# Reordering the spectral stage of a decoder kernel: correlation ahead of the lag transforms, two PSUM banks used differently, masked scores in PSUM

## The chip, the cores and the metric

The kernel runs on one core of one Trainium2 chip. The metric is the device time of one execution in microseconds, and each kernel is judged by the median of several runs. The engines are TensorE (PE; its weight loads are shown apart as PEld), VectorE (DVE), ScalarE (ACT) and GpSimd (POOL); SyncE (SP) issues the DMAs. Each engine works through its own list of instructions in order, and they meet only through semaphores.

## The reference

Everything is computed on 32 sequences of 64 tokens with 512 features, in float32:

```
x = x + attn_block(layernorm(x))      # dequantised weights + LoRA, then gate/up/down
x = x + autocorrelation(Q=layernorm(x), K=ctx, V=ctx)
x = x + top1_expert_lora(layernorm(x))

def autocorrelation(Q, K, V):         # 8 heads of 64 features, over the 64 positions
    corr = ifft(fft(q) * conj(fft(k))).real
    w, idx = top_k(corr, 8)           # per feature, over the lags
    w = softmax(w)
    out = sum_i w[i] * v[min(idx[i] + pos, L - 1)]
```

The last two lines of x, for 16 tiles of 128 tokens (two sequences each), are the spectral stage, which this change touches. The first line, some 690 us of the execution, is untouched.

## The kernel before, in words

The spectral stage is a software pipeline written out by hand. `slots` (L985) runs over slots v; in slot v an engine does stage s for tile t = v - s, so up to four tiles are under way. Each engine has its own `piece` function, from L1039 (SP), L1087 (POOL), L1156 (ACT), L1251 (DVE) and L1336 (PE), and the order of the calls there is the order of its queue. Nothing plans it: order and waits stand as written. Stage 0 of tile 0 runs earlier, between the last matmuls of the block before, so that the slots of PE, ACT, DVE and POOL begin at v = 1 and the last is v = 18.

Fourier transforms are matmuls by fixed 64-row matrices, one for each of the two sequences (`by_sequence`, L696, its matmuls on line L700). For one tile, in order:

- Stage 0. PE transforms ctx to kc (`pe_kc`) and ACT copies it out (`act_kc`, L739); PE transforms the normalised x (`pe_q`, from xq, which ACT made at L687); PE transforms ctx once more to kn (`pe_kn`), and ACT copies it (L745). DVE multiplies q by kc (`dve_product`, L755), and PE transforms back with the products as weights (`pe_corr`, L767). DVE takes the 8 largest of each row (`dve_top`, L782), subtracts the largest (L786, L788), ACT takes exponentials (`act_exp`, L803, L807), DVE sums (`dve_sum`, L813), POOL divides (`pool_divide`, L822, tile en), DVE marks the chosen lags (`dve_mark`, L797).
- Stage 1. DVE weighs (`dve_weigh`, L831, tile wl), PE transposes that (`pe_lags`, L843), ACT copies it to wts (`act_lags`, L865). PE transforms wts twice, `pe_cyclic` and `pe_negacyclic` (both L700); DVE multiplies the first by kc (`dve_cyclic`, L877), ACT copies the second (L871), and POOL multiplies it by kn (`pool_negacyclic`, L885, tile pn). PE transforms both products back into one sum (`pe_gather`, L896), and DVE adds x (`dve_x3`, L905).
- Stage 2. Layer norm of x3 (`dve_stats`, `pool_pow`, `dve_rstd`, ACT at L676), PE transposes it (`pe_turn_h`, L913), ACT copies it to x3t (L920), PE computes router logits and the low-rank products (`pe_route`, L928), DVE picks the expert (`dve_route`, L939 to L953: mx, sc, m2, rw, wh), PE transposes wh (`pe_turn_wh`, L960), ACT copies that to wht (`act_expert`, L971).
- Stage 3. PE multiplies wht by the expert matrix (`pe_expert`, L965), DVE adds it (`dve_final`, L977), and SP stores the tile.

PSUM has eight banks. CORR is bank 0, LAGS bank 1 (the transposed lags, and later in the same tile the gathered sum), QW banks 2 and 3 (q, then the cyclic transform), MISC bank 4 (transposed x, then the expert's output), ROUTE bank 5, KW banks 6 and 7 (kc, kn, negacyclic transform). A semaphore guards each reuse. PE's order in a slot is kc(v), q(v), lags(v-1), expert(v-3), kn(v), cyclic(v-1), negacyclic(v-1), corr(v), turn_h(v-2), route(v-2), gather(v-1) twice, turn_wh(v-2). The kn copy must precede the negacyclic transform, which writes over kn.

Of the kernel before, what the change touches and what calls it, by code (L numbers as in the profile page):

```python
# [97 lines left out]
def build(nc, x, ctx_in, codes, scale_nat, scale_rows, lora_attn, lora_h, lora_ft, lora_down_b,  # L98
# [91 lines left out]
    x3t = two("x3t")  # L190
    mx, sc, m2, rw = two("mx", (8,)), two("sc", (E,)), two("m2", (8,)), two("rw", (E,))
    wh, wht = two("wh", (P,)), two("wht", (P,))
# [5 lines left out]

    CORR, LAGS, QW, MISC, ROUTE, KW = 0, 1, 2, 4, 5, 6

# [509 lines left out]
    def pe_q(pe, t, b):  # L710
        pe.wait_ge(xq_done, t + 1)
        if t == 0:
            pe.wait_ge(kn_copied, 1)
        elif t == 1:
            pe.wait_ge(hmul_done, 2 * NG * NCH)
        else:
            pe.wait_ge(pcyc, t - 1)
        by_sequence(pe, q_bank(t), SPEC, xq[:, b]).then_inc(q_ready, 1)

    def pe_kc(pe, t, b, h):  # L720
        pe.wait_ge(ctx_in_s[b], 16 * h + 16)
        if t == 0:
            pe.wait_ge(const_in, 48)
            pe.wait_ge(folded, PER * NG)
        elif t == 1:
            pe.wait_ge(prod, 1)
        else:
            pe.wait_ge(wn_copied, t - 1)
        by_sequence(pe, KW, KCYC, ctx[:, b]).then_inc(kc_ready, 1)
# [45 lines left out]
    def dve_top(dve, t, b):  # L775

        corr = ps[:, CORR].rearrange("p (r l) -> p r l", l=L)
        dve.wait_ge(corr_ready, t + 1)
        if real(2 * (t - 1)):
            dve.wait_ge(exp_done, 2 * (t - 1))  # L780
# [28 lines left out]
    def dve_sum(dve, t, b):  # L809
        dve.wait_ge(exp_done, 2 * t + 1)  # L810
        if real(t - 1):
# [5 lines left out]
    def pool_divide(pool, t, b):  # L817
        pool.wait_ge(exp_done, 2 * t + 2)
        pool.wait_ge(summed, 2 * t + 2)
# [40 lines left out]
    def act_lags(act, t, b):  # L860
        act.wait_ge(lag_turned, t + 1)
        if real(t - 1):
            act.wait_ge(wc_ready, t - 1)
            act.wait_ge(wn_ready, t - 1)
        nc.scalar.copy(wts[:, b], ps[:, LAGS]).then_inc(lag_copied, 1)  # L865

# [20 lines left out]
    def pe_gather(pe, t, b, k):  # L887

        if k == 0:
            pe.wait_ge(lag_copied, t + 1)  # L890
            pe.wait_ge(pcyc, t + 1)
        else:
            pe.wait_ge(pneg, 2 * t + 2)
        mat, src = ((OUT, pc), (OUT_N, pn))[k]
        for s in range(2):
            mm = nc.tensor.matmul(ps[s * L:(s + 1) * L, LAGS], spec[:, mat, 0:L], src[:, b, s],  # L896
                                  start=(k == 0), stop=(k == 1))
# [3 lines left out]
    def dve_x3(dve, t, b):  # L901
        dve.wait_ge(gathered, t + 1)
        if real(t - 1):
            dve.wait_ge(fin_done, t - 1)
        nc.vector.tensor_tensor(x3[:, b], tile_of(acc, t), ps[:, LAGS], ALU.add).then_inc(x3_done, 1)  # L905

    def pe_turn_h(pe, t, b):
        pe.wait_ge(xh3_done, t + 1)
        if real(t):
            pe.wait_ge(fin_done, t)  # L910
        for j in range(KT):
# [20 lines left out]
    def dve_route(dve, t, b):  # L932

        logits = ps[:, ROUTE, P:P + E]
        n = 4 * t
        dve.wait_ge(routed_in, t + 1)
        if real(4 * (t - 1)):
# [3 lines left out]
        dve.wait_ge(prio_set, E)  # L941
        nc.vector.scalar_tensor_tensor(out=sc[:, b], in0=logits, scalar=mx[:, b, 0:1], in1=prio[:],
                                       op0=ALU.is_equal, op1=ALU.mult).then_inc(route, 1)
        dve.wait_ge(route, n + 2)
        nc.vector.max(m2[:, b], sc[:, b]).then_inc(route, 1)
        dve.wait_ge(route, n + 3)
        nc.vector.scalar_tensor_tensor(out=rw[:, b], in0=sc[:, b], scalar=m2[:, b, 0:1],
                                       in1=mx[:, b, 0:1].to_broadcast([P, E]), op0=ALU.is_equal,
# [35 lines left out]

    def slots(e, piece, first=1):  # L985


        for v in range(first, TT + DEEP):
            def at(stage):

                t = v - stage
                return (t, t % 2, t // 2) if 0 <= t < TT else None
            piece(at)
# [6 lines left out]
    with nc.Block() as block:  # L1000

        @block.sync
        def _(sp):
# [40 lines left out]
            slots(sp, piece, 0)  # L1044
            for b in range(2):
# [3 lines left out]
        def _(pool):  # L1049
# [37 lines left out]
            def piece(at):  # L1087
                if a := at(2):
                    pool_pow(pool, *a[:2])
                if a := at(1):  # L1090
                    pool_negacyclic(pool, *a[:2])
                if a := at(0):
                    pool_divide(pool, *a[:2])
            slots(pool, piece)

        @block.scalar
        def _(act):
# [20 lines left out]
            def body(g, gp, m, ahead):  # L1118
                for c in range(NCH):
# [19 lines left out]
                    else:  # L1139
# [12 lines left out]
            pairs(act, body)  # L1152
            act_exp(act, 0, 0)
            act.wait_ge(added, 4 * NCH * NG)

            def piece(at):  # L1156
                if a := at(0):
                    act_kc(act, *a[:2])
                if a := at(1):
                    act_lags(act, *a[:2])  # L1160
                if a := at(0):
                    act_kn(act, *a[:2])
# [4 lines left out]
                if a := at(2):  # L1167
                    act_turn_h(act, *a[:2])
                if a := at(-1):
                    act_normalise_x2(act, *a[:2])  # L1170
                if a := at(0):
                    act_exp(act, *a[:2])
# [5 lines left out]
        def _(dve):  # L1178
# [72 lines left out]
            def piece(at):  # L1251
                if a := at(1):
                    dve_weigh(dve, *a[:2])
                if a := at(2):
                    dve_stats(dve, *a[:2])
                if a := at(0):
                    dve_product(dve, *a[:2])
                if a := at(2):
                    dve_rstd(dve, *a[:2])
                if a := at(1):  # L1260
                    dve_cyclic(dve, *a[:2])
                if a := at(3):
                    dve_final(dve, *a)
                if a := at(0):
# [4 lines left out]
                if a := at(0):  # L1269
                    dve_mark(dve, *a[:2])  # L1270
# [5 lines left out]
        def _(pe):  # L1276
# [59 lines left out]
            def piece(at):  # L1336
                if a := at(0):
                    pe_kc(pe, *a)
                    pe_q(pe, *a[:2])
# [4 lines left out]
                if a := at(0):  # L1344
                    pe_kn(pe, *a[:2])
                if a := at(1):
                    pe_cyclic(pe, *a[:2])
                    pe_negacyclic(pe, *a[:2])
                if a := at(0):
                    pe_corr(pe, *a[:2])  # L1350
                if a := at(2):
                    pe_turn_h(pe, *a[:2])
                    pe_route(pe, *a[:2])
                if a := at(1):
                    pe_gather(pe, *a[:2], 0)
                    pe_gather(pe, *a[:2], 1)
                if a := at(2):
                    pe_turn_wh(pe, *a[:2])
            slots(pe, piece)
# [58 lines left out]
```

## Time and profile before

| | |
|---|---|
| median of 3 runs | 934.58 us (934.45, 934.58, 938.98) |
| the profiled execution | 935.97 us, span 934.2 us |
| busy over the span | PE 827.9, DVE 567.6, ACT 393.4, POOL 205.2 us |
| TensorE clock granted over the span | 0.97 |
| span of the spectral stage | from 691 us to the end |

The profile is of one execution. Each row of a timeline gives the start, the duration, the engine, the line of the code, the operation with its output and inputs, their shapes, how many instructions are merged into it, and in brackets how long the engine was idle before it and which instruction released it. Tiles are named without their buffer numbers; ps is any PSUM bank. "issue" is idle time for which the profile shows no releaser. A granted clock of 1.00 is 2.4 GHz.

### The profile page before, as it was taken

The page shows a single profiled execution, that of the slowest core. Times are in us where ns is not written, and L with a number is a line of the kernel's source. Part 1 is how long each engine was busy: PE and PEld are TensorE (multiplying, and loading weights), DVE is VectorE, ACT ScalarE, POOL GpSimd, SP SyncE. Part 2 cuts the span into 40 slices and gives each one's busy share as a digit, 9 for nine tenths or more (in the row PEclk, how much of TensorE's full clock was granted, in tenths as well). Part 3 has the DMA queues.
Part 4 walks back from the last instruction along what each step waited for, and adds up shares of the span by engine and source line. Part 5 has one row for each costly group of instructions (what it writes and reads, how often), then busy time and mean ns, then how long its engine had stood idle before and what let it go on. Part 6 is the DMA issues. An engine that isn't in the chain of part 4 may idle for free. (4 is left out here: it accounts for less than half of the span.)

```text
span 934.2 us, 10840 instructions
## 1 busy us (share of the span) xinstructions
PE 827.9 (89%) x3548; PEld 574.4 (61%) x3548; DVE 567.6 (61%) x1327; ACT 393.4 (42%) x675; POOL 205.2 (22%) x187
## 2 busy tenths in 40 slices
PE   2577769899999999999999999999968888888875
PEld 0233357677777777777777777787744434444432
DVE  3777556665456456456456456423467788787783
ACT  3666545544344344444443443211214444544431
POOL 2000001122222222222222222222113323223221
PEclk9799989999999999999999999999979999999997
DMA  5422111211111111111112111010000101101100
GB/s 157 127 71 78 45 51 31 69 49 50 45 49 49 46 47 50 46 39 58 46 38 61 46 38 45 1 66 1 11 1 12 45 24 46 46 24 46 39 19 34
DMA packets 26551, 43.06 MB, mean 46 GB/s; under 512 B 4368, under 2 KB 6576, under 8 KB 26496
## 3 DMA queue, kind: packets, MB, share of 16 engines
q1 hardware_dynamic: 26496, 42.37, 14.7%
q8 instruction: 29, 0.48, 0.2%
q14 instruction: 26, 0.21, 0.1%
HBM read 38.16 MB, written 4.19 MB: 45 GB/s over the span
## 5 line engine op out<-in xcount | busy, mean ns | idle before, releaser
L478 PE MATMUL ps<-x_hi,w_hi 128*128 128x512 f32 x448 | 189.9, 424 | 2.4 <-DVE x_lo L526 2.4
L480 PE MATMUL ps<-x_hi,w_lo 128*128 128x512 f32 x448 | 175.4, 392 | 0.0
L479 PE MATMUL ps<-x_lo,w_hi 128*128 128x512 f32 x448 | 175.1, 391 | 0.0
L602 DVE TENSOR_TENSOR acc<-acc,ps 128x512 f32<-128x512 f32 x112 | 75.7, 685 | 78.8 <-PE ps L480 78.8
L365 POOL TENSOR_TENSOR w_lo<-wt,w_hi 128x512 fp32r<-128x512 f32 x42 | 54.7, 1303 | 274.7 <-ACT w_hi L360 274.7
L593 POOL TENSOR_TENSOR h_lo<-hf,h_hi 128x512 fp32r<-128x512 f32 x56 | 72.1, 1287 | 177.7 <-ACT h_hi L588 177.4
L478 PEld LDWEIGHTS ps<-x_hi,w_hi 128*128 128x128 f32 x448 | 84.3, 188 | 30.2 <-issue 13.9
L581 DVE TENSOR_TENSOR hf<-hf,ps 128x512 f32<-128x512 f32 x56 | 38.4, 687 | 101.1 <-PE ps L480 101.1
L479 PEld LDWEIGHTS ps<-x_lo,w_hi 128*128 128x128 f32 x448 | 84.4, 188 | 25.2 <-issue 8.7
L480 PEld LDWEIGHTS ps<-x_hi,w_lo 128*128 128x128 f32 x448 | 84.4, 188 | 18.0
L575 ACT ACTIVATE hf<-ps 128x512 f32<-128x512 f32 x56 | 33.5, 597 | 143.7 <-PE ps L480 143.7
L478 PE MATMUL ps<-w_hi,h_hi 128*128 128x512 f32 x224 | 88.3, 394 | 4.1 <-DVE acc L602 4.1
L588 ACT CAST h_hi<-hf 128x512 fp32r<-128x512 f32 x56 | 34.7, 620 | 129.0 <-DVE hf L581 128.9
L479 PE MATMUL ps<-w_lo,h_hi 128*128 128x512 f32 x224 | 88.1, 393 | 0.0
L480 PE MATMUL ps<-w_hi,h_lo 128*128 128x512 f32 x224 | 88.0, 393 | 0.0
L453 PE MATMUL ps<-w,wt 128*128 128x512 f32 x96 | 49.1, 659 | 16.1 <-DVE wt L305 9.7
L885 POOL TENSOR_TENSOR pn<-wns,kn 128x512 f32<-128x512 f32 x32 | 40.0, 1270 | 73.8 <-ACT wns L871 73.8
L284 DVE SCALAR_TENSOR_TENSOR piece_c<-piece_c,piece_a 128x512 f32<-128x512 f32 x58 | 41.1, 709 | 22.2 <-ACT piece_c L273 18.4
L287 DVE SCALAR_TENSOR_TENSOR piece_d<-piece_d,piece_c 128x512 f32<-128x512 f32 x58 | 52.9, 912 | 2.0
L280 DVE SCALAR_TENSOR_TENSOR piece_a<-piece_a,piece_b 128x512 f32<-128x512 f32 x58 | 47.5, 819 | 10.7 <-ACT piece_b L267 10.1
L478 PEld LDWEIGHTS ps<-w_hi,h_hi 128*128 128x128 f32 x224 | 42.6, 190 | 13.4 <-issue 4.5
L351 DVE TENSOR_TENSOR wt<-wt,ps 128x512 f32<-128x512 f32 x42 | 28.7, 682 | 35.6 <-PE ps L320 35.6
(120 smaller groups left out, 1378.4 us busy)
## 6 DMA issues: line engine op xcount, KB each, us to landing
codes_sb<-in_codes SPq DMA_DIRECT2D x58, 256.0 KB, 2.6
scale_sb<-in_scale_rows SPq DMA_DIRECT2D x92, 128.0 KB, 2.9
acc<-in_x SPq DMA_DIRECT2D x4, 1024.0 KB, 5.8
ctx<-in_ctx SPq DMA_DIRECT2D x16, 256.0 KB, 2.6
out<-fin SPq DMA_DIRECT2D x16, 256.0 KB, 2.0
lft<-in_lora_ft SPq DMA_DIRECT2D x56, 16.0 KB, 1.9
spec<-in_spectral SPq DMA_DIRECT2D x1, 448.0 KB, 3.3
rt<-in_router SPq DMA_DIRECT2D x1, 272.0 KB, 3.6
```

The source lines that it names most:

```text
L280: nc.vector.scalar_tensor_tensor(out=piece_a[:, b], in0=piece_a[:, b], scalar=KA, in1=piece_b[:, b], op0=ALU.add, op1=ALU.min).then_inc(mi ...
L284: nc.vector.scalar_tensor_tensor(out=piece_c[:, b], in0=piece_c[:, b], scalar=-SHIFT, in1=piece_a[:, b], op0=ALU.add, op1=ALU.min).then_in ...
L287: nc.vector.scalar_tensor_tensor(out=piece_d[:, b], in0=piece_d[:, b], scalar=KD, in1=piece_c[:, b], op0=ALU.add, op1=ALU.max).then_inc(mi ...
L365: nc.gpsimd.tensor_tensor(w_lo[gp][:, k], wt[:, b], w_hi[gp][:, k].bitcast(F32), ALU.subtract).then_inc(lo_done, 1)
L453: mm = nc.tensor.matmul(ps[:, kt, :], wt[:, u % 2, kt * P:(kt + 1) * P], w3[:, o], start=(u == KT), stop=False)
L478: nc.tensor.matmul(bank, hi, rhs_hi, start=start, stop=False)
L479: nc.tensor.matmul(bank, hi, rhs_lo, start=False, stop=False)
L480: return nc.tensor.matmul(bank, lo, rhs_hi, start=False, stop=stop)
L581: nc.vector.tensor_tensor(hf[:, i], hf[:, i], ps[:, 2 * i + 1], ALU.mult).then_inc(hmul_done, 1)
L593: nc.gpsimd.tensor_tensor(h_lo[:, c % 2, i], hf[:, i], h_hi[:, c % 2, i].bitcast(F32), ALU.subtract).then_inc(hlo_done, 1)
L602: nc.vector.tensor_tensor(tile, tile, ps[:, 4 + s % 2], ALU.add).then_inc(added, 1)
L885: nc.gpsimd.tensor_tensor(pn[:, b, s], wns[:, b, s], kn[:, b, s], ALU.mult).then_inc(pneg, 1)
```

## The change

What it does, part by part:

- The transposed lags go to bank MISC instead of bank 1, and bank 1 (now named GATHER) holds only the gathered sum. `pe_lags` waits for the x3t copy of an earlier tile instead of for x3; `pe_gather` waits for x3; and `pe_expert(v-3)`, which writes MISC, waits for the wts copy of tile v-1.
- PE's new order is kc(v), q(v), turn_wh(v-3), lags(v-1), expert(v-3), kn(v), corr(v), negacyclic(v-1), cyclic(v-1), turn_h(v-2), route(v-2), gather twice. So turn_wh moves into the next slot.
- DVE's new order is weigh, product, stats, rstd, final, top, cyclic, sum, route, mark, x3.
- ACT's order is the same; the exponential of the top values has a semaphore of its own, `top_exp`.
- The masked scores sc of `dve_route` are in PSUM (bank ROUTE) instead of SBUF.
- SP loads ctx a slot earlier. POOL's calls are written in another order with other stages (`pool_pow` for tile v-1 at the end of slot v instead of tile v-2 at its start), which gives the same queue.

```diff
-    CORR, LAGS, QW, MISC, ROUTE, KW = 0, 1, 2, 4, 5, 6
+    CORR, GATHER, QW, MISC, ROUTE, KW = 0, 1, 2, 4, 5, 6
...
-    def act_exp(act, t, b):
+    def act_exp_top(act, t, b):
         act.wait_ge(topd_done, t + 1)
         flat = topd[:, b].rearrange("p r k -> p (r k)")
-        nc.scalar.activation(flat, flat, ACT.Exp).then_inc(exp_done, 1)
+        nc.scalar.activation(flat, flat, ACT.Exp).then_inc(top_exp, 1)
+
+    def act_exp(act, t, b):
         act.wait_ge(less_done, t + 1)
...
     def dve_sum(dve, t, b):
-        dve.wait_ge(exp_done, 2 * t + 1)
+        dve.wait_ge(top_exp, t + 1)
...
     def pe_lags(pe, t, b):
...
-        if real(t):
-            pe.wait_ge(x3_done, t)
+        if real(t - 1):
+            pe.wait_ge(h_copied, t - 1)
...
-            mm = nc.tensor.transpose(ps[:, LAGS, ch], wl[:, b, ch], eye[:])
+            mm = nc.tensor.transpose(ps[:, MISC, ch], wl[:, b, ch], eye[:])
...
     def pe_gather(pe, t, b, k):
         if k == 0:
-            pe.wait_ge(lag_copied, t + 1)
             pe.wait_ge(pcyc, t + 1)
+            if real(t):
+                pe.wait_ge(x3_done, t)
...
     def dve_route(dve, t, b):
         logits = ps[:, ROUTE, P:P + E]
+        sc = ps[:, ROUTE, 3 * P:3 * P + E]
...
     def pe_expert(pe, t, b):
         pe.wait_ge(wh_copied, t + 1)
-        pe.wait_ge(h_copied, t + 1)
+        pe.wait_ge(lag_copied, min(t + 3, TT))
...
```

The calls of DVE's `piece` (L1251):

```diff
                 if a := at(1):
                     dve_weigh(dve, *a[:2])
+                if a := at(0, 1):
+                    dve_product(dve, *a[:2])
                 if a := at(2):
                     dve_stats(dve, *a[:2])
-                if a := at(0):
-                    dve_product(dve, *a[:2])
                 if a := at(2):
                     dve_rstd(dve, *a[:2])
+                if a := at(3):
+                    dve_final(dve, *a)
+                if a := at(0, 1):
+                    dve_top(dve, *a[:2])
                 if a := at(1):
                     dve_cyclic(dve, *a[:2])
-                if a := at(3):
-                    dve_final(dve, *a)
-                if a := at(0):
-                    dve_top(dve, *a[:2])
+                if a := at(0, 1):
                     dve_sum(dve, *a[:2])
...
```

The calls of PE's `piece` (L1336):

```diff
+                if a := at(0, 1):
                     pe_q(pe, *a[:2])
+                if a := at(3):
+                    pe_turn_wh(pe, *a[:2])
                 if a := at(1):
                     pe_lags(pe, *a[:2])
                 if a := at(3):
                     pe_expert(pe, *a[:2])
-                if a := at(0):
+                if a := at(0, 1):
                     pe_kn(pe, *a[:2])
+                if a := at(0, 1):
+                    pe_corr(pe, *a[:2])
+                if a := at(1):
+                    pe_negacyclic(pe, *a[:2])
                 if a := at(1):
                     pe_cyclic(pe, *a[:2])
-                    pe_negacyclic(pe, *a[:2])
-                if a := at(0):
-                    pe_corr(pe, *a[:2])
                 if a := at(2):
                     pe_turn_h(pe, *a[:2])
                     pe_route(pe, *a[:2])
                 if a := at(1):
                     pe_gather(pe, *a[:2], 0)
                     pe_gather(pe, *a[:2], 1)
-                if a := at(2):
-                    pe_turn_wh(pe, *a[:2])
```

`at(stage, first)` gives tile v - stage if it is at least `first` and exists; with `first` = 1 it leaves out tile 0, whose stage 0 has run earlier.

## Rows read from the trace of the kernel before

**Rows 1.** Windows view, ten slots: us, busy us (count) per engine, clock, DMA.

```profile
750.10:891.60 141.50, 122.43 (x633) 62.31 (x632) 115.14 (x452) 67.85 (x100) 40.84 (x40) 1.00 0.11 38
```

**Rows 2.** Timeline of PE, one slot: start us, us, engine, line, operation [idle before].

```profile
806.41 0.33 PE L960 MATMUL ps<-eye,wh 128*128 128x128 f32 x1 [0.39 <-DVE wh L953]
806.67 1.13 PE L700 MATMUL ps<-ctx,spec 64*128 64x512 f32 x4
...
809.19 0.66 PE L843 MATMUL ps<-eye,wl 128*128 128x128 f32 x4 [0.54 <-DVE wl L831]
809.68 1.02 PE L965 MATMUL ps<-eb,wht 128*128 128x512 f32 x2
810.64 1.13 PE L700 MATMUL ps<-ctx,spec 64*128 64x512 f32 x4
811.60 1.02 PE L700 MATMUL ps<-wts,spec 64*128 64x512 f32 x4
812.93 1.13 PE L700 MATMUL ps<-wts,spec 64*128 64x512 f32 x4 [0.30 <-issue]
813.99 2.00 PE L767 MATMUL ps<-spec,pp 128*128 128x64 f32 x16
815.82 0.60 PE L913 MATMUL ps<-eye,xh 128*128 128x128 f32 x4
817.10 1.19 PE L928 MATMUL ps<-rt,x3t 128*128 128x136 f32 x8 [0.68 <-ACT x3t L920]
818.23 1.08 PE L896 MATMUL ps<-pc,spec 128*64 128x512 f32 x4
819.13 1.03 PE L896 MATMUL ps<-pn,spec 128*64 128x512 f32 x4
...
820.80 0.70 PE L700 MATMUL ps<-ctx,spec 64*128 64x512 f32 x2
```

**Rows 3.** Timeline of ACT, the same slot.

```profile
806.77 0.27 ACT L971 COPY wht<-ps 128x128 f32<-128x128 f32 x1 [1.89 <-PE ps L960]
807.84 1.01 ACT L739 COPY kc<-ps 128x1024 f32<-128x1024 f32 x1 [0.80 <-PE ps L700]
809.88 0.58 ACT L865 COPY wts<-ps 128x512 f32<-128x512 f32 x1 [1.03 <-PE ps L843]
811.82 1.01 ACT L745 COPY kn<-ps 128x1024 f32<-128x1024 f32 x1 [1.34 <-PE ps L700]
...
814.09 1.01 ACT L871 COPY wns<-ps 128x1024 f32<-128x1024 f32 x1 [0.56 <-PE ps L700]
816.46 0.59 ACT L920 COPY x3t<-ps 128x512 f32<-128x512 f32 x1 [1.36 <-PE ps L913]
816.94 0.82 ACT L687 ACTIVATE xq<-acc,nmr,rstd 128x512 f32<-128x512 f32 x1
```

**Rows 4.** Timeline of DVE, the same slot and the next slot's first weighing.

```profile
816.02 1.15 DVE L782 MAX8 top<-ps 128x8 f32<-128x64 f32 x8 [1.53 <-PE ps L767]
...
818.28 0.20 DVE L813 TENSOR_REDUCE zs<-topd 128x8 f32<-128x64 f32 x1
...
819.27 0.89 DVE L947 SCALAR_TENSOR_TENSOR rw<-sc,m,mx 128x8 f32<-128x8 f32 x1
...
822.59 0.68 DVE L831 SCALAR_TENSOR_TENSOR wl<-mark,en 128x512 f32<-128x512 f32 x1
```

**Rows 5.** Timeline of POOL, the same slot.

```profile
815.18 2.49 POOL L885 TENSOR_TENSOR pn<-wns,kn 128x512 f32<-128x512 f32 x2 [4.41 <-ACT wns L871]
819.10 1.04 POOL L822 TENSOR_TENSOR en<-ex,rz 128x512 f32<-128x512 f32 x1 [1.42 <-ACT ex L807]
```

**Rows 6.** Instructions of line L947: count, ns min/median/max, first and last start.

```profile
L947 DVE SCALAR_TENSOR_TENSOR rw<-sc,m,mx x16: 225/891/953, 720.3 to 927.5; 128x8 f32<-128x8 f32 x16
```

**Rows 7.** Instructions of line L602, same columns.

```profile
L602 DVE TENSOR_TENSOR acc<-acc,ps x112: 677/687/689, 210.8 to 691.1; 128x512 f32<-128x512 f32 x112
```

**Rows 8.** Timeline of PE in the first slot of the stage.

```profile
698.95 2.08 PE L700 MATMUL ps<-ctx,spec 64*128 64x512 f32 x4
```

More of the change, by code:

```diff
@@ L190, in build @@
     x3t = two("x3t")
-    mx, sc, m2, rw = two("mx", (8,)), two("sc", (E,)), two("m2", (8,)), two("rw", (E,))
+    mx, m2, rw = two("mx", (8,)), two("m2", (8,)), two("rw", (E,))
     wh, wht = two("wh", (P,)), two("wht", (P,))
@@ L636, in build @@
     marked, exp_done, summed, divided = sem("marked"), sem("exp_done"), sem("summed"), sem("divided")
+    top_exp = sem("top_exp")
     weighed, lag_turned, lag_copied = sem("weighed"), sem("lag_turned"), sem("lag_copied")
@@ L715, in pe_q @@
             pe.wait_ge(hmul_done, 2 * NG * NCH)
+        elif t > 1:
+            pe.wait_ge(pcyc, t - 1)
         else:
-            pe.wait_ge(pcyc, t - 1)
+            pe.wait_ge(prod, t)
         by_sequence(pe, q_bank(t), SPEC, xq[:, b]).then_inc(q_ready, 1)
@@ L726, in pe_kc @@
             pe.wait_ge(prod, 1)
+        elif t > 1:
+            pe.wait_ge(wn_copied, t - 1)
         else:
-            pe.wait_ge(wn_copied, t - 1)
+            pe.wait_ge(kn_copied, t)
         by_sequence(pe, KW, KCYC, ctx[:, b]).then_inc(kc_ready, 1)
@@ L778, in dve_top @@
         dve.wait_ge(corr_ready, t + 1)
-        if real(2 * (t - 1)):
-            dve.wait_ge(exp_done, 2 * (t - 1))
+        if real(t - 1):
+            dve.wait_ge(exp_done, t - 1)
         for r in range(8):
@@ L817, in pool_divide @@
     def pool_divide(pool, t, b):
-        pool.wait_ge(exp_done, 2 * t + 2)
+        pool.wait_ge(exp_done, t + 1)
         pool.wait_ge(summed, 2 * t + 2)
@@ L864, in act_lags @@
             act.wait_ge(wn_ready, t - 1)
-        nc.scalar.copy(wts[:, b], ps[:, LAGS]).then_inc(lag_copied, 1)
+        nc.scalar.copy(wts[:, b], ps[:, MISC]).then_inc(lag_copied, 1)
     def act_negacyclic(act, t, b):
@@ L895, in pe_gather @@
         for s in range(2):
-            mm = nc.tensor.matmul(ps[s * L:(s + 1) * L, LAGS], spec[:, mat, 0:L], src[:, b, s],
+            mm = nc.tensor.matmul(ps[s * L:(s + 1) * L, GATHER], spec[:, mat, 0:L], src[:, b, s],
                                   start=(k == 0), stop=(k == 1))
@@ L904, in dve_x3 @@
             dve.wait_ge(fin_done, t - 1)
-        nc.vector.tensor_tensor(x3[:, b], tile_of(acc, t), ps[:, LAGS], ALU.add).then_inc(x3_done, 1)
+        nc.vector.tensor_tensor(x3[:, b], tile_of(acc, t), ps[:, GATHER], ALU.add).then_inc(x3_done, 1)
     def pe_turn_h(pe, t, b):
         pe.wait_ge(xh3_done, t + 1)
-        if real(t):
-            pe.wait_ge(fin_done, t)
+        if real(t + 0):
+            pe.wait_ge(fin_done, t + 0)
         for j in range(KT):
@@ L941, in dve_route @@
         dve.wait_ge(prio_set, E)
-        nc.vector.scalar_tensor_tensor(out=sc[:, b], in0=logits, scalar=mx[:, b, 0:1], in1=prio[:],
+        nc.vector.scalar_tensor_tensor(out=sc, in0=logits, scalar=mx[:, b, 0:1], in1=prio[:],
                                        op0=ALU.is_equal, op1=ALU.mult).then_inc(route, 1)
         dve.wait_ge(route, n + 2)
-        nc.vector.max(m2[:, b], sc[:, b]).then_inc(route, 1)
+        nc.vector.max(m2[:, b], sc).then_inc(route, 1)
         dve.wait_ge(route, n + 3)
-        nc.vector.scalar_tensor_tensor(out=rw[:, b], in0=sc[:, b], scalar=m2[:, b, 0:1],
+        nc.vector.scalar_tensor_tensor(out=rw[:, b], in0=sc, scalar=m2[:, b, 0:1],
                                        in1=mx[:, b, 0:1].to_broadcast([P, E]), op0=ALU.is_equal,
@@ L983, in build, with slots, at @@
     DEEP = 3
-    def slots(e, piece, first=1):
-        for v in range(first, TT + DEEP):
-            def at(stage):
+    def slots(e, piece):
+        for v in range(TT + DEEP):
+            def at(stage, first=0):
                 t = v - stage
-                return (t, t % 2, t // 2) if 0 <= t < TT else None
+                return (t, t % 2, t // 2) if first <= t < TT else None
             piece(at)
@@ L1039, in piece @@
             def piece(at):
-                if a := at(0):
+                if a := at(-1, 2):
                     sp_ctx(sp, a[0], a[1])
@@ L1043, in piece @@
                     sp_store(sp, a[0], a[1])
-            slots(sp, piece, 0)
+            for t in range(2):
+                sp_ctx(sp, t, t)
+            slots(sp, piece)
             for b in range(2):
@@ L1152, in _ @@
             pairs(act, body)
+            act_exp_top(act, 0, 0)
             act_exp(act, 0, 0)
@@ L1168, in piece @@
                     act_turn_h(act, *a[:2])
-                if a := at(-1):
+                if a := at(-1, 2):
                     act_normalise_x2(act, *a[:2])
-                if a := at(0):
+                if a := at(0, 1):
+                    act_exp_top(act, *a[:2])
+                if a := at(0, 1):
                     act_exp(act, *a[:2])
@@ L1268, in piece @@
                     dve_route(dve, *a[:2])
-                if a := at(0):
+                if a := at(0, 1):
                     dve_mark(dve, *a[:2])
@@ L1336, in piece @@
             def piece(at):
-                if a := at(0):
+                if a := at(0, 1):
                     pe_kc(pe, *a)
+                if a := at(0, 1):
                     pe_q(pe, *a[:2])
+                if a := at(3):
+                    pe_turn_wh(pe, *a[:2])
                 if a := at(1):
@@ L1343, in piece @@
                     pe_expert(pe, *a[:2])
-                if a := at(0):
+                if a := at(0, 1):
                     pe_kn(pe, *a[:2])
+                if a := at(0, 1):
+                    pe_corr(pe, *a[:2])
+                if a := at(1):
+                    pe_negacyclic(pe, *a[:2])
                 if a := at(1):
                     pe_cyclic(pe, *a[:2])
-                    pe_negacyclic(pe, *a[:2])
-                if a := at(0):
-                    pe_corr(pe, *a[:2])
                 if a := at(2):
                     pe_turn_h(pe, *a[:2])
+                if a := at(2):
                     pe_route(pe, *a[:2])
```

9 lines of the change are left out of this document (5 added, 4 removed).

## The prediction

> **What bounds the kernel now.** I read the windows view first: in ten slots of the spectral stage the tensor engine is busy 122 of 141.5 us at a granted clock of 1.00 (its 2.4 GHz level), VectorE 115, ScalarE 68, GpSimd 41 [rows 1]. No engine is full, so waits decide, and they repeat every 14.13 us (the kc transform starts at 806.67 and again at 820.80) [rows 2]. All times below are of that slot, whose tile in stage 0 I call v.
>
> Then I laid the timelines of the engines side by side. The loop that closes is: VectorE weighs (822.59 less a slot, so 808.45), PE transposes (809.19), expert (809.68), kn (810.64), ScalarE copies kn (811.82 to 812.83), only then PE's negacyclic transform (812.93), then the correlation (813.99), and VectorE, idle for 1.53, starts the maxima at 816.02 and works without a gap to the next weighing at 822.59 [rows 2 to 4]. Summed: 0.74 + 0.49 + 0.96 + 1.18 + 1.11 + 1.06 + 2.03 + 6.57 = 14.14. Two things in it invite the change: the correlation stands behind two lag transforms and a wait for ScalarE, and the routing's rw operation takes 0.89 for 8 columns, ending just when GpSimd's en ends (819.27 + 0.89 = 820.16; 819.10 + 1.04 = 820.14). Where GpSimd is idle, at the end, the same rw takes 225 ns; it has two SBUF inputs [rows 4 to 6]. Operations with one input in PSUM, as the 112 accumulations, stay at 677 to 689 ns though GpSimd works beside many of them [rows 7].
>
> By the Trainium skill, "SBUF — State Buffer", section "Who interferes with whom", a VectorE instruction with two SBUF inputs blocks against a GpSimd one that reads SBUF, and one with at most one such input does not. By that rule the masked scores in PSUM free rw, and nothing new is blocked; the opposite case is rival C below.
>
> **The change, part by part.** I lay out the new slot from K, the start of kc(v) on PE. One pitch is the start of an instruction group to the earliest start of the next.
>
> *ScalarE's queue.* Its order is unchanged, but the transpose of wh for tile v-3 moves from the end of one slot to behind kc and q of the next, while the copy of its result (wht) stays the last thing of the old slot, so it stands in front of the kc copy. What is queued behind it: the kc copy, then the wts copy. Before, kc was copied at 807.84, 1.17 after kc started, and ended a full 1.03 before wts was wanted (809.88) [rows 2, 3]. Now: q at K+0.96 (kn to cyclic has the same form and pitch), transpose of wh at K+1.91, wht copy 0.36 later at K+2.27, duration 0.27. Back to back, ScalarE starts the next 0.11 before the last ends (x3t 0.59, next start 0.48 later) [rows 3]. So the kc copy starts at K+2.43 (bounds: 2.38 and 2.60) and the wts copy at K+3.33, ending at K+3.92.
>
> *The shared bank.* The lag transposes now go to the bank that expert writes, so expert waits for the wts copy: new wait, and kn, correlation and everything behind stand in PE's queue behind it. Expert starts at K+3.97. Before, it ran under that copy.
>
> *PE's order.* Then pitches from rows 2: a group whose weight load is exposed lasts 1.13 instead of 1.02 (kc, kn, neg against cyclic, expert), and the next starts 0.07 before its end. Expert 1.06, kn 1.06, correlation 2.00 - 0.07 = 1.93, neg 0.96, cyclic 0.95, up to the transposes of xh: K+3.97 + 5.96 = K+9.93. From there 0.69 to the x3t copy (as lags to wts, exposed), 0.59 + 0.05 to route: K+11.26; route 1.13, gather0 0.90, gather1 0.96: the next kc at K+14.25. Against the 14.13 of now that is +0.12 for each slot.
>
> The low end of this chain is 14.05, if the two added changes between matmuls on 64 and 128 rows (kn to correlation, correlation to neg) expose no weight load and the kc copy starts at 2.38; the high end is 14.45, if each exposes twice what kc does. The Trainium skill, "TensorEngine Tiling (Array Packing)", "Key Properties", says that changing the tiling mode drains the engine; by that too two more changes a slot would cost, which speaks against the change.
>
> *What the other queues do in the new slot.* The product pp starts when kc is copied, K+3.5, and is done at 4.7, before the correlation at 6.09. The maxima start at 6.09 + 2.03 = K+8.12. From maxima to the sum is 2.26 now, with the product pc in between some 1.2 more (two banks; one bank takes 0.68 to 0.69 [rows 7], so under 1.4) [rows 4]: K+11.6 to 11.8. But the sum waits for the exponentials, and ScalarE issues those behind x3t (K+10.62 to 11.21) and the normalisation xq (0.82), so at K+11.82 to 12.1. From sum to weighing takes 822.59 - 818.28 = 4.31, less the stall of rw (0.89 - 0.23 = 0.66 [rows 6]): 3.65, so K+15.75, or 1.5 after the next kc. The lags then start at 2.24 after it and could be copied at 2.93; ScalarE is free for them only at 3.33. So the VectorE loop has 0.4 of slack, and the 0.66 saved in rw buys nothing more. GpSimd: neg at K+8.0, its copy at 9.2, pn 1.09 after that for 2.49 [rows 2, 3, 5]: done at 12.8, gather1 wanted at 13.3; hidden with 0.5 to spare, at a cost of what exceeds it. The gather's own bank, the split semaphore of the exponentials and the ctx load issued a slot earlier on SP cost nothing: each only loosens a wait; the ctx load, behind kn of the tile before, has a slot more to land. GpSimd's order is the same as before written in another way. The new PSUM destination costs at most the difference between its neighbours of 8 columns; 0.1 either way, under the slack.
>
> *Fill.* In slots 1 and 2 there is no wht copy and no expert, so there the correlation in front does pay. kn of slot 1 runs 698.95 to 701.03 [rows 8]; then the correlation at 700.96, neg 702.89, its copy 704.05, pn 705.14 to 707.64, gather1, and kc(2) at 708.7. With no wht copy, slot 2 is: q 0.96, lags 0.95, kn 0.58, 1.06, 1.93, 0.96, 0.95, 0.69, 0.64, 1.13, 0.90, 0.96 = 11.7: kc(3) at 720.4. Before, it is 806.67 less six slots: 721.8. Fill -1.4 (bounds -2.2 and -0.6).
>
> *Drain.* The last weighing comes 1.50 after kc instead of 808.45 - 806.67 = 1.78 [rows 2, 4], -0.3; expert's wait gives 0.4 back and neg in front of cyclic takes up to 0.9 off the way to pn. I take -0.4 (bounds -1.2 and +0.5).
>
> *Sum.* 13 slots (3 to 15) x (+0.12) = +1.5; fill -1.4; drain -0.4: -0.3 on the profiled execution's 935.97, whose span is 934.2. The median of the runs is 934.58, 1.39 below that execution, and I carry the difference over: **934.3**.
>
> **The rivals.**
> B, faster: the wht copy does not hold up the kc copy in effect, say because the two meet differently in time. Then the wts copy starts when the lags are there, and the VectorE loop decides: 0.74 + 0.69 + 0.64 + 1.06 + 1.06, from the correlation 6.05 to the sum (neg, cyclic, transposes, x3t, xq, exponential) and 3.65 = 13.87. 13 x (-0.26) = -3.4, fill -1.4, drain -0.4, in all -5.2: 929.4. For it: the maxima come 2 us nearer to the weighing. Against: the code's order leaves no room.
> C, slower: GpSimd holds up VectorE whatever the inputs. The sum then waits for pn's end (0.7 late), and rw for en, which follows it: another 0.3 to 0.5. Beyond the slack of 0.4 that is +0.6 to +0.7 a slot: 13 x 0.77 with the 0.12 above = +10.0, -1.8: 942.8. It decides from 0.4 of stall a slot. Against: one SBUF input did not stall in any accumulation [rows 7].
> D, the PSUM scores don't free rw: it ends with en at K+13.9, 0.57 late, 0.17 over the slack: 13 x 0.29 = +3.8, -1.8: 936.6.
>
> **How the numbers follow.** Forecast 0.60, B 0.22, C 0.10, D 0.08. The forecast's own bounds, 13 slots between 14.05 and 14.45 with those of fill and drain, add up to 930.2 and 938.7; all at one end is unlikely, so 931 to 938 is its own range. To take in half of B and part of C I give 928.5 to 939. About 0.5% (4.7 us) is what a measurement tells from no change. Faster: most of B and a little of the forecast, 0.20. Slower: C and the forecast's far end, 0.14. Same 0.66.
>
> **What would show it.** Right: the kc copy starts right behind the wht copy, 2.4 after kc; wts copied about 3.3 after kc; expert right behind that; PE idle about 1.2 before expert; slot 14.1 to 14.4; rw at 0.23; VectorE idle before the maxima near zero and before the sum some 0.5. Wrong: kc copied 1.2 after kc starts (B); the sum or rw long beside GpSimd (C, D); or a slot under 13.9 or over 14.6.

## The result, and the profile after

| | before | changed |
|---|---|---|
| median of the runs | 934.71 us (20 runs) | 939.37 us (20 runs) |
| ratio, 95% interval | | 1.0044 (1.0033 to 1.0055) |
| profiled execution, its span | 935.97, 934.2 us | 939.26, 937.5 us |
| kc(1) to kc(3), the fill (kc(n) is the start of kc of tile n on PE) | 30.77 us | 31.07 us |
| one slot, steady (12 slots, kc(3) to kc(15)) | 14.15 us | 14.35 us |
| kc(15) to the end of the span | 42.6 us | 42.25 us |

The change made the kernel slower, by 4.1 us by the ratio (3.1 to 5.1) and 4.66 by the medians. The forecast was 934.3, with 939.0 as the end of its range; the measured 939.37 lies outside. The spans differ by 3.3: 0.90 because the stage began later in this execution (691.94 against 691.04; over the thirteen executions profiled here it began anywhere from 688.3 to 693.9, with the code in front of it unchanged, so I count it as scatter), 0.30 in the fill, 12 slots x 0.206 = 2.47 up to kc(15), and -0.37 after that. Twelve slots of 0.206 are thus only part of the 4.1 us; the fill is the part that differs most between executions, as the runs below show. The other 19 runs of the changed kernel have no trace; their granted clock over the span was 0.961 to 0.970, in the median 0.966 where the profiled one had 0.969. That would fit a longer fill in most of them, but it isn't shown.

The windows view of ten slots of the changed kernel, the same columns as [rows 1], says that they are longer with the clock still at 1.00: VectorE is less busy than before, PE's matmuls nearly the same (12.5 us a slot against 12.2).

```profile
723.01:866.54 143.53, 124.82 (x632) 62.89 (x630) 107.45 (x449) 63.72 (x100) 40.52 (x40) 1.00 0.11 38
```

One slot of the changed kernel on PE, to be laid beside [rows 2]; the first line is kc, the last but one the second gather, the last the next kc.

```profile
809.13 1.13 PE L701 MATMUL ps<-ctx,spec 64*128 64x512 f32 x4
...
811.05 0.33 PE L969 MATMUL ps<-eye,wh 128*128 128x128 f32 x1
811.46 0.66 PE L850 MATMUL ps<-eye,wl 128*128 128x128 f32 x4
813.23 1.10 PE L974 MATMUL ps<-eb,wht 128*128 128x512 f32 x2 [1.12 <-ACT wts L872]
814.26 1.13 PE L701 MATMUL ps<-ctx,spec 64*128 64x512 f32 x4
815.32 2.00 PE L772 MATMUL ps<-spec,pp 128*128 128x64 f32 x16
817.25 1.99 PE L701 MATMUL ps<-wts,spec 64*128 64x512 f32 x8
819.16 0.66 PE L921 MATMUL ps<-eye,xh 128*128 128x128 f32 x4
820.50 1.19 PE L936 MATMUL ps<-rt,x3t 128*128 128x136 f32 x8 [0.68 <-ACT x3t L928]
...
822.53 1.03 PE L904 MATMUL ps<-pn,spec 128*64 128x512 f32 x4
823.49 0.70 PE L701 MATMUL ps<-ctx,spec 64*128 64x512 f32 x2
```

ScalarE at the head of the same slot, against [rows 3]:

```profile
811.42 0.27 ACT L980 COPY wht<-ps 128x128 f32<-128x128 f32 x1 [3.95 <-PE ps L969]
811.58 1.02 ACT L744 COPY kc<-ps 128x1024 f32<-128x1024 f32 x1
812.48 0.60 ACT L872 COPY wts<-ps 128x512 f32<-128x512 f32 x1
```

VectorE, against [rows 4], and then GpSimd's division, against [rows 5]:

```profile
812.69 1.23 DVE L760 TENSOR_TENSOR pp<-ps,kc 128x1024 f32<-128x1024 f32 x1 [1.29 <-issue]
...
817.35 1.15 DVE L787 MAX8 top<-ps 128x8 f32<-128x64 f32 x8 [0.43 <-PE ps L772]
...
821.33 0.22 DVE L820 TENSOR_REDUCE zs<-topd 128x8 f32<-128x64 f32 x1 [0.83 <-ACT topd L808]
...
822.42 0.23 DVE L956 SCALAR_TENSOR_TENSOR rw<-ps,m,mx 128x8 f32<-128x8 f32 x1
...
825.07 0.68 DVE L838 SCALAR_TENSOR_TENSOR wl<-mark,en 128x512 f32<-128x512 f32 x1
```

```profile
821.98 1.04 POOL L829 TENSOR_TENSOR en<-ex,rz 128x512 f32<-128x512 f32 x1
```

What to see: the wht copy waits for PE's transpose (idle 3.95) and the kc copy starts in its wake, 2.45 after kc instead of 1.17. The wts copy follows without a pause, and only behind it does PE go on with expert, after 1.12 idle. The correlation does reach VectorE sooner (idle 0.43 instead of 1.53) and rw is down to 0.23 beside a running en, but the sum now waits 0.83 for the exponential. The time taken out at one place came back at two others: in front of expert and in front of the sum.

The fill of the changed kernel on PE: kn(1), the two gathers of tile 0, kc(2), q(2).

```profile
699.84 2.08 PE L701 MATMUL ps<-ctx,spec 64*128 64x512 f32 x4
...
707.12 1.08 PE L904 MATMUL ps<-pc,spec 128*64 128x512 f32 x4 [1.33 <-DVE pc L884]
708.62 1.89 PE L904 MATMUL ps<-pn,spec 128*64 128x512 f32 x4 [0.43 <-POOL pn L892]
710.44 1.97 PE L701 MATMUL ps<-ctx,spec 64*128 64x512 f32 x4
712.25 1.02 PE L701 MATMUL ps<-xq,spec 64*128 64x512 f32 x4
```

The second gather took 1.89 instead of the 1.03 of a steady slot and kc(2) 1.97 instead of 1.13; in the kernel before, both ran at full clock there (1.08 and 1.13). The granted clock there, in the windows view (the figure before the last two):

```profile
698.00:702.00 4.00, 3.20 (x9) 1.37 (x10) 1.88 (x3) 0.62 (x2) 0.00 (x0) 0.57 0.00 0
...
706.00:710.00 4.00, 2.46 (x8) 0.41 (x8) 2.94 (x19) 1.37 (x3) 3.50 (x3) 0.84 0.00 0
710.00:714.00 4.00, 4.00 (x16) 1.67 (x16) 1.73 (x3) 1.12 (x2) 0.00 (x0) 0.73 0.00 0
```

Between 702 and 706 it was 1.00. A level of 0.50 is 1.2 GHz, 1.00 is 2.4 GHz; PE had been idle from 693.9 to 698.8, and again 1.33 and 0.43 before the gathers.

### The profile page after: what moved, and what is told of

The parts are those of the page before. It is cut to its first block and busy times, and to the rows that moved or that the text cites. A ratio compares the mean times of both kernels' runs of the same rounds, so it can differ in the third digit from the quotient of the medians.

```text
span 937.5 us, 10838 instructions
## 1 busy us (share of the span) xinstructions
PE 828.8 (88%) x3548; PEld 573.7 (61%) x3548; DVE 557.0 (59%) x1327; ACT 387.8 (41%) x675; POOL 205.2 (22%) x187
## 5 line engine op out<-in xcount | busy, mean ns | idle before, releaser
L602 DVE TENSOR_TENSOR acc<-acc,ps 128x512 f32<-128x512 f32 x112 | 75.7, 686 | 78.2 <-PE ps L480 78.2
```

Source lines behind the costliest of these rows:

```text
L602: nc.vector.tensor_tensor(tile, tile, ps[:, 4 + s % 2], ALU.add).then_inc(added, 1)
```

## The experiments

Slot and fill of each are differences of the starts of kc in its one profiled execution. Each median is of 4 to 12 runs; ratio and interval compare all of them with 17 to 23 runs of the kernel before made beside them (medians 934.67 and 934.79), and need not be the quotient of the medians. The changed kernel's median is 939.37, its ratio 1.0044 (1.0033 to 1.0055).

| kernel | median us | ratio to before (95%) | slot | kc(1) to kc(3) |
|---|---|---|---|---|
| e1, transpose of wh back at the slot's end | 934.02 | 1.0002 (0.9987 to 1.0016) | 14.00 | 32.3 |
| e2, wht copy behind kc copy | 933.62 | 0.9982 (0.9966 to 0.9998) | 14.00 | 32.0 |
| e3, lags in bank 1 | 919.59 | 0.9838 (0.9824 to 0.9852) | 13.00 | 32.0 |
| e4, scores in SBUF | 939.93 | 1.0054 (1.0036 to 1.0072) | 14.40 | 32.0 |
| b1, before + scores in PSUM | 924.57 | 0.9888 (0.9869 to 0.9906) | 13.49 | 31.0 |
| b2, the order alone | 924.57 | 0.9896 (0.9879 to 0.9912) | 13.40 | 31.3 |
| f1, changed + filler at the gather | 939.77 | 1.0036 (1.0019 to 1.0054) | 14.35 | 32.5 |
| f3, e3 + filler at lags and gather | 915.68 | 0.9790 (0.9772 to 0.9808) | 13.00 | 28.0 |
| h1, changed + filler at lags and gather | 935.30 | 1.0005 (0.9992 to 1.0018) | 14.35 | 28.0 |
| h2, before + filler at lags | 932.33 | 0.9976 (0.9956 to 0.9996) | 14.14 | 29.35 |
| g1, best try | 908.05 | 0.9712 (0.9690 to 0.9733) | 12.45 | not comparable, kc is moved |

**e1.** PE's `piece`:

```diff
-                if a := at(3):
-                    pe_turn_wh(pe, *a[:2])
...
                     pe_gather(pe, *a[:2], 1)
+                if a := at(2):
+                    pe_turn_wh(pe, *a[:2])
```

> The changed kernel with one edit: PE transposes wh at the end of the slot, where it stood before the change. Theory 1 (the slot of 14.36 us is the chain kc, q, transpose of wh, wht copy, kc copy, wts copy, expert, and the rest of PE's list): the kc copy starts 1.2 after kc, the wts copy no longer waits for it, and the VectorE loop takes over at about 14.0: 13 slots x -0.36 = some -4.5 us against the changed kernel. Theory 2 (the slot is set by PE's own list, with the weight loads exposed at six changes between 64 and 128 rows): slot stays at 14.3 or more, time within 1 us of the changed kernel.

ScalarE in this kernel (kc starts at 804.55):

```profile
804.66 0.27 ACT L980 COPY wht<-ps 128x128 f32<-128x128 f32 x1 [2.03 <-PE ps L969]
805.73 1.01 ACT L744 COPY kc<-ps 128x1024 f32<-128x1024 f32 x1 [0.81 <-PE ps L701]
807.31 0.58 ACT L872 COPY wts<-ps 128x512 f32<-128x512 f32 x1 [0.56 <-PE ps L850]
```

The kc copy starts 1.18 after kc, and the wts copy waits 0.56 for the lags and no longer for ScalarE. The slot is 14.00, as theory 1 had it, and the median 5.4 us under the changed kernel, where 4.5 was expected. Theory 2 falls.

**e2.** ScalarE's `piece`:

```diff
                 if a := at(0, 1):
                     act_kc(act, *a[:2])
+                if a := at(3):
+                    act_expert(act, *a[:2])
...
-                if a := at(2):
-                    act_expert(act, *a[:2])
             slots(act, piece)
```

> The changed kernel with one edit on ScalarE only: the wht copy stands behind the kc copy of the next slot instead of in front of it; PE's list is untouched. Theory 1: kc copied 1.2 after kc, wht copy behind it, wts copy when the lags are there (2.9 to 3.0 after kc instead of 3.35), slot about 14.0, -4.5 us against the changed kernel, the same as moving the transpose. Theory 2: no difference.

```profile
806.07 1.01 ACT L744 COPY kc<-ps 128x1024 f32<-128x1024 f32 x1 [2.85 <-PE ps L701]
807.18 0.27 ACT L980 COPY wht<-ps 128x128 f32<-128x128 f32 x1
807.91 0.58 ACT L872 COPY wts<-ps 128x512 f32<-128x512 f32 x1 [0.47 <-PE ps L850]
```

The same slot with PE's list untouched. So it was not where PE transposes wh that cost, but that the copy of it stood in front of kc's in another engine's queue.

**e3.** The bank part undone:

```diff
     def pe_lags(pe, t, b):
-        if real(t - 1):
-            pe.wait_ge(h_copied, t - 1)
+        if real(t):
+            pe.wait_ge(x3_done, t)
...
-            mm = nc.tensor.transpose(ps[:, MISC, ch], wl[:, b, ch], eye[:])
+            mm = nc.tensor.transpose(ps[:, GATHER, ch], wl[:, b, ch], eye[:])
...
-        nc.scalar.copy(wts[:, b], ps[:, MISC]).then_inc(lag_copied, 1)
+        nc.scalar.copy(wts[:, b], ps[:, GATHER]).then_inc(lag_copied, 1)
...
     def pe_gather(pe, t, b, k):
         if k == 0:
+            pe.wait_ge(lag_copied, t + 1)
             pe.wait_ge(pcyc, t + 1)
-            if real(t):
-                pe.wait_ge(x3_done, t)
...
     def pe_expert(pe, t, b):
-        pe.wait_ge(lag_copied, min(t + 3, TT))
+        pe.wait_ge(h_copied, t + 1)
```

> The changed kernel with the bank part undone: the transposed lags share bank 1 with the gathered sum again (lags wait for x3, gather for the wts copy) and expert doesn't wait for the wts copy. Theory 1 (expert's wait for the wts copy carries all behind it): expert runs under the copy, kn starts 1.4 us earlier relative to kc, and the slot falls to 13.0 to 13.3, where the loop from the weighing over kn, correlation, x3t and the exponential closes: 13 x -1.2 = -14 to -17 us against the changed kernel, about 923 us, faster than both. Theory 2: slot stays over 14.2.

PE in this kernel: kc, lags, expert, kn, correlation, and the next kc.

```profile
799.39 1.13 PE L701 MATMUL ps<-ctx,spec 64*128 64x512 f32 x4
...
801.72 0.66 PE L850 MATMUL ps<-eye,wl 128*128 128x128 f32 x4
802.21 1.02 PE L973 MATMUL ps<-eb,wht 128*128 128x512 f32 x2
803.16 1.13 PE L701 MATMUL ps<-ctx,spec 64*128 64x512 f32 x4
804.22 2.00 PE L772 MATMUL ps<-spec,pp 128*128 128x64 f32 x16
...
812.39 1.13 PE L701 MATMUL ps<-ctx,spec 64*128 64x512 f32 x4
```

Expert follows 0.49 after the lags, as before the change, and kn starts 3.77 after kc instead of 5.13. The slot falls to 13.00, with the wht copy still in front of the kc copy, and the kernel is 1.6% faster than before. The shared bank was the dearest part of the change: 1.35 a slot. The fall of 19.8 us is more than I expected (14 to 17). In the two spans, which differ by 20.0, the twelve slots up to kc(15) give 16.0 and the stretch behind it 2.4 (39.9 instead of 42.25); the rest is that the stage began 2.6 earlier in this execution, against a fill 1.0 longer.

**e4.** The masked scores back in SBUF:

```diff
-        sc = ps[:, ROUTE, 3 * P:3 * P + E]
+        sc = scs[:, b]
```

> The changed kernel with the masked scores sc back in SBUF. If the VectorE stall beside GpSimd comes from the two SBUF inputs, rw takes about 0.6 again (it would start 0.4 into the 1.03 of en) and the weighing comes 0.4 later; ScalarE's queue has 0.3 to 0.4 of slack over it, so the slot grows by at most 0.1: 0 to +1.5 us against the changed kernel. If GpSimd stalls VectorE whatever the inputs, there is no difference in rw, 0.23 in both.

```profile
806.86 0.64 DVE L956 SCALAR_TENSOR_TENSOR rw<-sc,m,mx 128x8 f32<-128x8 f32 x1
```

rw takes 0.64 instead of 0.23, ending just behind en (807.50 against 806.42 + 1.05 = 807.47), and the slot grows by 0.05, to 14.40: the slack on ScalarE hides nearly all of it. In time it can't be told from the changed kernel (939.93 against 939.37, the intervals overlap).

**b1.** The same edit made alone on the kernel before:

```diff
+        sc = ps[:, ROUTE, 3 * P:3 * P + E]
...
-        nc.vector.scalar_tensor_tensor(out=sc[:, b], in0=logits, scalar=mx[:, b, 0:1], in1=prio[:],
+        nc.vector.scalar_tensor_tensor(out=sc, in0=logits, scalar=mx[:, b, 0:1], in1=prio[:],
...
-        nc.vector.max(m2[:, b], sc[:, b]).then_inc(route, 1)
+        nc.vector.max(m2[:, b], sc).then_inc(route, 1)
...
-        nc.vector.scalar_tensor_tensor(out=rw[:, b], in0=sc[:, b], scalar=m2[:, b, 0:1],
+        nc.vector.scalar_tensor_tensor(out=rw[:, b], in0=sc, scalar=m2[:, b, 0:1],
```

> The kernel before with one edit: the masked scores sc in PSUM. There rw's stall of 0.66 stands on the loop that closes at 14.14 (VectorE works without a gap from the maxima to the weighing). Theory 1: rw 0.23, the slot falls by the whole 0.66 to 13.48: 13 x -0.66 = -8.6 us, about 926. Theory 2 (stalls whatever the inputs): rw stays at 0.9, no change.

```profile
801.21 0.23 DVE L948 SCALAR_TENSOR_TENSOR rw<-ps,m,mx 128x8 f32<-128x8 f32 x1
...
810.60 2.50 POOL L885 TENSOR_TENSOR pn<-wns,kn 128x512 f32<-128x512 f32 x2 [4.42 <-ACT wns L871]
...
812.62 0.56 DVE L786 TENSOR_TENSOR topd<-top 128x64 f32<-128x64 f32 x1
```

rw is 0.23 and the slot 13.49: here the whole 0.65 comes off. That is 7.6 us up to kc(15); from there to the end it is 39.3 instead of 42.6, so the 10.2 us of the medians are more than the 8.6 expected. topd, whose two inputs are both in SBUF, still takes 0.56 and ends at 813.18, just behind GpSimd's pn (813.10); in the changed kernel, where GpSimd is idle at that moment, it takes 0.23. By the Trainium skill, "SBUF — State Buffer", "Who interferes with whom", a VectorE instruction with two SBUF inputs contends with a GpSimd instruction that reads SBUF, and one with at most one such input, outside the 2-port modes, does not. These rows agree with it, in both directions.

**b2.** The order part alone: e3 and e1 and e4 together, that is, the changed order of correlation, lag transforms and VectorE's calls over the old banks.

> The order part alone: the changed kernel's orders of PE and VectorE, but the transpose of wh, the banks and the masked scores as before the change. Theory 1: neither the wht copy nor expert's wait holds anything; the loop from the weighing is 0.74 + 0.49 + 0.95 + 1.06 + 3.84 + 0.70 + 0.48 + 0.72 + 0.27 + 3.74, and rw's stall of 0.43 on top = 13.4: 13 x -0.72 = -9.4 us and some fill, about 925. Theory 2 (the new order itself costs through more changes between 64 and 128 rows): over 14.1, no faster than before.

Slot 13.40, 924.57 us, as expected. The order in itself is worth 10 us; so are the scores in themselves. The two don't add up: with both, the lags in bank 1 and the transpose of wh moved (e3), the kernel is 15 us faster than before and not 20.

**f1.** The fill. In front of the first gather of tile 0:

```diff
+        if t == 0:
+            for _ in range((2, 0)[k]):
+                nc.tensor.matmul(ps[:, ROUTE], eye[:], eb[:], start=True, stop=True)
```

> The changed kernel plus two matmuls of 128 by 512 in front of the first gather of slot 1, where PE idles 1.33 us; their result goes to an unused bank. The changed kernel's second gather and kc(2) ran at the lower clock (1.89 and 1.97 us instead of 1.03 and 1.13). Theory 1 (the idle PE lets the clock fall, and that ate the gain forecast for slots 1 and 2): both at full clock, kc(3) comes 1.5 to 1.8 us earlier after kc(1), time -1.7 us against the changed kernel. Theory 2 (the clock falls for another reason): the same half-speed groups, no gain, up to +0.5 us.

```profile
698.00 2.08 PE L701 MATMUL ps<-ctx,spec 64*128 64x512 f32 x4
700.01 3.67 PE L772 MATMUL ps<-spec,pp 128*128 128x64 f32 x16
...
710.86 1.13 PE L701 MATMUL ps<-ctx,spec 64*128 64x512 f32 x4
```

I had the wrong idle stretch. In this execution the correlation of slot 1 took 3.67 instead of 2.00 and the two lag transforms behind it ran at the lower clock too: it was low already before the filler. kc(2) ran at full speed, but so it did without filler in e1 to e4. kc(1) to kc(3) is 32.5, no gain where 1.7 was expected. The other profiles of the new order without filler have 32.0 to 32.3 (e1 to e4) and 31.3 (b2), so the 31.07 of the changed kernel's profile is the short end.

**f3.** e3 with the filler of f1 and five more matmuls in front of the first lag transposes, where PE idles 4.9 us while VectorE finishes the statistics and the weighing:

```diff
     def pe_lags(pe, t, b):
-        pe.wait_ge(weighed, t + 1)
         if t == 0:
             pe.wait_ge(added, 4 * NCH * NG)
+            for _ in range(5):
+                nc.tensor.matmul(ps[:, ROUTE], eye[:], eb[:], start=True, stop=True)
+        pe.wait_ge(weighed, t + 1)
```

> The changed kernel with the lags in bank 1 (slot 13.0) plus filler matmuls in slot 1: five in front of the first lag transposes (PE idles 4.9 us there, and the kn behind it took 2.08 instead of 1.13) and two in front of the first gather. Theory 1 (idle PE, lower clock): lags, kn, gather and kc(2) at full clock, -2.5 to -3 us against the kernel without filler (919.6), about 917. Theory 2: no gain, up to +1 us.

kc(1) to kc(3) falls from 32.0 to 28.0, and the time by 3.9 us, more than the 2.5 to 3 expected.

**h1.** Both fillers in the changed kernel.

> The changed kernel, all of it, plus filler matmuls in slot 1 in front of the first lag transposes (five) and of the first gather (two). Slots stay at 14.36. Theory 1 (what ate the gain forecast for slots 1 and 2 is the lower clock after PE's idle 4.9 us): kc(1) to kc(3) falls from 31.1 in the changed kernel's profile to 28 as in the kernel with filler and the lags in bank 1, time -3 to -4 us against the changed kernel, about 935.7. Theory 2: it stays within 1 us of the changed kernel.

PE: the filler, kn(1), the second gather of tile 0, kc(2); then the windows view.

```profile
695.78 4.56 PE L846 MATMUL ps<-eb,eye 128*128 128x512 f32 x10
...
701.30 1.13 PE L701 MATMUL ps<-ctx,spec 64*128 64x512 f32 x4
...
709.12 1.08 PE L909 MATMUL ps<-pn,spec 128*64 128x512 f32 x4
710.13 1.13 PE L701 MATMUL ps<-ctx,spec 64*128 64x512 f32 x4
```

```profile
698.00:702.00 4.00, 3.62 (x14) 1.48 (x12) 2.56 (x7) 0.58 (x1) 1.01 (x1) 1.00 0.00 0
...
706.00:710.00 4.00, 4.00 (x14) 1.07 (x12) 3.43 (x20) 1.86 (x4) 3.44 (x3) 1.00 0.00 0
```

The clock is 1.00 throughout, gather 1.08 and kc(2) 1.13; the fill is 28.0, the median 4.1 us less. The lags start 6.86 after kc(1), as without filler, so the filler held nothing up. f1 shows that the two matmuls at the gather do nothing alone; whether the five in front of the lags would have been enough in the new order was not run.

**h2.** The filler in front of the lags, in the kernel before.

> The kernel before, plus five filler matmuls in front of the first lag transposes. Theory 1 says that in the old order the slower slot 1 costs less, since PE waits there for ScalarE's kn copy and for pn anyway: kn 1.13 instead of 2.08, the chain kn, kn copy, negacyclic, correlation some 1 to 1.5 us shorter, -1 to -1.5 us. If the clock costs both orders the same, -3 to -4 us.

kc(1) to kc(3) is 29.35 instead of 30.77, -1.4 and within the expectation; the medians fall by 2.5 (ratio 0.9976, 0.9956 to 0.9996).

**g1.** A version made from what the runs say: e3, both fillers, e2, and

```diff
-                if a := at(0, 1):
+                if (a := at(0, 1)) and a[0] == 1:
                     pe_kc(pe, *a)
...
                 if a := at(2):
                     pe_turn_h(pe, *a[:2])
+                if a := at(-1, 2):
+                    pe_kc(pe, *a)
...
+                if a := at(0, 1):
+                    dve_mark(dve, *a[:2])
                 if a := at(2):
                     dve_route(dve, *a[:2])
-                if a := at(0, 1):
-                    dve_mark(dve, *a[:2])
...
-                if a := at(-1, 2):
-                    act_normalise_x2(act, *a[:2])
                 if a := at(0, 1):
                     act_exp_top(act, *a[:2])
                 if a := at(0, 1):
                     act_exp(act, *a[:2])
+                if a := at(-1, 2):
+                    act_normalise_x2(act, *a[:2])
```

> A version made of what the runs point to: the changed kernel with the lags in bank 1, filler in slot 1, the wht copy behind the kc copy, kc of the next tile transformed by PE in the gap between the transposes of xh and the routing, VectorE's marking in front of the routing, ScalarE's exponentials in front of the next normalisation. By the same bookkeeping PE's list is 12.2 without its 0.8 gap and the weighing loop 12.3 without the wait for the routing matmuls: slot 12.3 to 12.5, 13 x -0.6 = -7 to -9 us against 915.7, about 907 to 909. If a wait that I don't see closes first, the slot stays at 12.8 to 13.0 and the time within 3 us of 915.7.

PE, from the transposes of xh over the next tile's kc and route to q:

```profile
803.64 0.65 PE L925 MATMUL ps<-eye,xh 128*128 128x128 f32 x4
804.23 1.13 PE L701 MATMUL ps<-ctx,spec 64*128 64x512 f32 x4
805.29 1.19 PE L940 MATMUL ps<-rt,x3t 128*128 128x136 f32 x8
...
808.28 1.13 PE L701 MATMUL ps<-xq,spec 64*128 64x512 f32 x4
```

kc fills the gap in which PE waited for x3t, route follows without idle time, and the slot is 12.45: 908.05 us, 2.9% under the kernel before.

## Why the prediction was wrong, point by point

*ScalarE's queue.* Right. kc copy at K+2.45 (2.43 forecast), wts copy at 3.35 (3.33). e1 and e2 show that this order costs 0.35 a slot.

*The shared bank.* The mechanism was right, and it is the dearest part (e3, 1.35 a slot). Its size was a little off: expert resumed at K+4.10, not 3.97. I had given PE 0.05 from the end of a ScalarE copy to the next weight load; here it took 0.12 (813.08 to 813.20, expert's matmul at 813.23), and the two copies ran 0.01 to 0.02 longer.

*PE's order.* Every pitch from expert on held within 0.03: kn, correlation, lag transforms at K+5.13, 6.19, 8.12, transposes at 10.03, the next kc at 14.36. Each is 0.10 later than forecast, all of it from expert. The two added changes between 64 and 128 rows cost 0.10 each, as the forecast had it: kn to the next group is 1.06 where it was 0.96 [rows 2], the correlation to the next 1.93 where it was 1.83. The correlation's first weight load now starts with the group (both 815.32), where that of the group behind kn had begun 0.21 ahead of it (811.39 against 811.60). So the slot was 14.35 instead of 14.25, inside its bounds. The 12 slots grew by 0.206 each and not by 0.12, so 12 or 13 of them are 1.0 to 1.1 us of the miss.

*The other queues.* Right: VectorE's loop, pn and the PSUM scores stayed under the slack; e4 puts the scores at 0.05 a slot here, and b1 at 0.65 where there is no slack.

*Fill.* This is the step that failed. I forecast -1.4 and wrote every group from 700.96 on at its full-clock length, a fill of 29.4. The profile had 31.07, +0.30 on the kernel before instead of -1.4, and the other executions of the new order without the filler at the lags between +0.5 and +1.7. The 1.67 over the forecast is two groups: the second gather with 1.89 where 1.08 is its length at full clock (h1), and kc(2) with 1.97 for 1.13, together 1.65. With the clock at 1.00 in both kernels (h1, h2) the fill is 28.0 against 29.35: -1.35, the forecast.

What took the place of the forecast is the clock: PE is idle for 4.9 us ahead of the first lag transposes, the level is low behind that, and the new order pays more for it. The old order lost 1.42 by it in the profile of before (30.77 to 29.35), the new one 3.07 in its profile and 4.0 in those of e2 to e4, always against the 28.0. In the profiles of before and of the changed kernel the loss is, within 0.06, just the sum of what the slower groups took more (1.48 and 3.07), so hardly any of it was hidden by another wait. Where the level was low once and for long, the old order (b1) was back at full clock when its correlation came (2.00), and kc(2) came 2.1 later than with filler (17.69 after kc(1), h2 15.59); in the new order, where the correlation stands right behind kn, the correlation ran at the low level too (3.67 instead of 2.00 in f1 and e4), and kc(2) came 4.0 later (20.3 in e4 against 16.27 in h1).

The sign of it stood in [rows 8], kn at 2.08; I used that figure and took the clock as recovered from there. I gave the fill bounds of -2.2 to -0.6, and none of them held the clock.

*Drain.* Forecast -0.4, with the +0.12 of slot 15 -0.28; measured -0.37 for the two: right.

*Rivals.* B did not happen because nothing takes the wht copy from in front of the kc copy; when e1 and e2 took it away, B's slot came out, 14.00 instead of 13.87 (expert's 0.1 again). C is refuted by rw's 0.23 beside en, and D as well. The sum: +1.1 from the slots and +1.7 in the fill (+2.7 where it went as in e2 to e4) turn the forecast -0.3 into +2.5 to +3.5; the interval of the ratio is +3.1 to +5.1, the medians differ by 4.66. So up to some 2 us are not accounted for by the profiles; how much of that is the scatter of the stage's start isn't shown. What stays open too is why the level falls once and for long in some executions and twice for short in others; no run here separates that.

## What to carry to other kernels

When an operation is moved on one engine, look at where its consumer stands in the other engine's queue: a transpose moved some 2 us later on PE held up its copy on ScalarE, and with it the two copies queued behind it (kc and wts). Two tiles that share a PSUM bank can add a wait to every pass; ask what else is queued behind the waiting instruction (here kn, the correlation and both lag transforms) before saving a bank. And for the first slots of a pipeline, read the granted clock and the length of the same group in a steady slot before using its full-clock length.

## What the runs showed of the hardware

Three parts of one change were worth, each alone on the kernel before or out of the changed one, -10 us (order, b2), -10 us (scores in PSUM, b1) and +20 us (the shared bank, e3); a fourth, the moved transpose of wh, cost 5 us beside the shared bank (e1). Together they made +4: what a part is worth depends on which others are there. The scores show it best: their stall of 0.66 us a slot weighs 10 us where VectorE closes the loop, while the 0.41 that it came to in e4, where ScalarE's queue closes it, could not be told from nothing.

Filler matmuls that compute nothing took 3.9 us off one kernel, 4.1 off another and some 2.5 off the kernel before by keeping the granted clock at 1.00 over a wait of 4.9 us. They held up nothing, since PE was idle there: the lags started 6.86 after kc(1) with them and without.
